# A graph network's three gather passes: block sums by one flat scan over feature-major rows in PSUM instead of chained steps

## Chip, core and metric

The kernel runs on 1 core of one Trainium2 chip. The metric is the device time of one execution in microseconds (us); the program before takes 11177.78 us, the median of 3 runs. Engines: PE is TensorE (matmul), DVE VectorE, ACT ScalarE, POOL GpSimd, SP SyncE.

## The reference

Four residual layers with a layer norm after each, over a graph of 12500 nodes with 64 features and 200000 edges, sorted by their destination `dst`. The last two layers gather rows by `src` and sum them by `dst`, which is what the three passes of this study do:

```
def gcn_conv(x, edge_index, W, b, num_nodes):        # layer 3, twice: passes c1 and c2
    norm = dinv[src] * dinv[dst]
    h = x @ W
    msg = h[src] * norm[:, None]
    out = jax.ops.segment_sum(msg, dst, num_segments=num_nodes)
    return out + b
# layer 4, attention with 4 heads of 16: pass at
attn = a_src_node[src] + a_dst_node[dst] + e_score
attn = jnp.where(attn >= 0, attn, NEG_SLOPE * attn)
attn_max = jnp.zeros((n, H), attn.dtype).at[dst].max(attn)
attn = jnp.exp(attn - attn_max[dst])
attn_sum = jnp.zeros((n, H), attn.dtype).at[dst].add(attn)
attn = attn / (attn_sum[dst] + EPS_SOFTMAX)
msg = h[src] * attn[:, :, None]
out = jnp.zeros((n, H, HD), h.dtype).at[dst].add(msg).reshape(n, OUT_DIM)
```

## The kernel before, in words

The sorted edges are cut into 128 runs, one per partition, of 1568 edges each. A pass goes through its run in NBLK = 98 blocks of J = 16 edges. Since edges of one destination are neighbours, a segment sum is a running sum that a flag resets: `same_dst` holds 1 where an edge has the destination of the edge before it, else 0, and a state is `old * flag + row`. The states of all edges go to DRAM (`states_c`, `states_at`), and after the pass POOL fetches, for each node, the state of its last edge.

The engines of passes c1 and c2 (D = 64 features), and of at (W3 = 68: 4 heads of 16 features and a 17th column, which carries the score and then the exponential; W3S = 72 with the running maximum of each head):

- **POOL** (line 641) issues 16 indirect DMAs a block, each of which gathers one row of the table per partition into `gb[r]`, one of R = 4 buffers. It takes a buffer again when the counter `state` says that the block that was there is summed.
- **DVE**, passes c1 and c2 (`conv`, line 1495): 16 SCALAR_TENSOR_TENSOR a block, each 128x64, each waiting for the one before by the semaphore `chain`; they write `st[h]`, and the last one counts up `state`. DVE itself starts a block when its 16 gathers have landed.
- **DVE**, pass at: L1616 to L1625 copy the maxima out, scale the state carried over and weigh the gathered rows by the exponentials (1024 elements a partition, in place in SBUF). `sums_of` then sums the 16 rows of 68 by a tree of joins (line 1425, 33 short instructions a block), with `run`, products of flags prepared before pass c1 (L1526, L1528). Between its levels stand the steps of the next block's scores (`score_step`, L1582 to L1605), two of which are short scans (L1597, L1601) with the flag rows `msk`.
- **ACT**, pass at: the edges' turned attributes (L689), `msk` (L681) and the exponentials (L701, L703), both in SBUF. In c1 and c2 ACT has nothing to do.
- **SP** (line 507) stores each block's states when `state` allows.

At a pass's end POOL waits for the stores, fixes the rows at the run borders (L599, L603) and fetches the nodes' rows (L610). Before pass at, DVE makes four scans over 1568 elements (L1563).

## Time and profile before

| what | us |
|---|---|
| time, median of 3 runs (lowest, highest) | 11177.78 (11177.54, 11199.18) |
| the profiled execution, span from first to last instruction | 11181.7 |
| busy in that span: POOL / DVE / PE / ACT | 7106.9 / 4736.9 / 1801.6 / 1142.1 |
| pass c1, from 3850 to 6018 | 2168 |
| pass c2, from 6222 to 8390 | 2168 |
| pass at, from 8707 to 10967 | 2260 |

A pass is counted from the start of its first gather to the end of its last. The profile lists no other time of the profiled execution than its span, which lies 3.9 us above the median. The three passes are 6596 us of the 11182; of the rest, about 3850 us are before c1 and are not touched.

### The profile page before, as it was taken

How to read it: one execution, taken by the hardware profiler on the slowest of the kernel's cores; microseconds unless marked ns; L12 is line 12 of the kernel's file. 1: busy time of each engine (PE TensorE's matmuls, PEld its weight loads, DVE VectorE, ACT ScalarE, POOL GpSimd, SP SyncE). 2: the span in 40 equal slices, each digit the busy share in tenths (PEclk: the TensorE clock that was granted, in tenths of full speed). 3: DMA queues.
4: the chain of work that ended last, by engine and by line, in shares of the span. 5: the costliest groups of instructions: out<-in, count | busy, mean ns of one | idle time of the engine just before them, and what ended most of it. 6: DMA issues, size and time to landing. Idle time of an engine off the chain costs nothing.

```text
span 11181.7 us, 57120 instructions
## 1 busy us (share of the span) xinstructions
PE 1801.6 (16%) x9285; PEld 1516.5 (14%) x9285; DVE 4736.9 (42%) x20005; ACT 1142.1 (10%) x2728; POOL 7106.9 (64%) x6884
## 2 busy tenths in 40 slices
PE   8744444444000400000000000000001000000000
PEld 7633333333000300000000000000000000000000
DVE  8855555555797422222221222222224344444446
ACT  0143434343000100000000000000000000000000
POOL 0566666666201377777776677777777776666766
PEclk7755555555555555555555555555555555555555
DMA  5144444444575111111111111111111222222221
GB/s 224 57 129 122 129 124 126 124 127 122 204 273 203 32 50 46 48 46 48 46 48 37 50 46 48 46 48 46 48 46 30 54 53 58 53 58 55 56 55 44
DMA packets 570444, 911.29 MB, mean 81 GB/s; under 512 B 333435, under 2 KB 348228, under 8 KB 544824
## 3 DMA queue, kind: packets, MB, share of 16 engines
q1 hardware_dynamic: 350264, 652.74, 17.3%
q0 software_dynamic: 219904, 255.88, 10.8%
q14 instruction: 226, 1.85, 0.1%
q8 instruction: 50, 0.82, 0.0%
HBM read 494.12 MB, written 414.02 MB: 81 GB/s over the span
## 4 chain that ended last, share of the span: by engine, by line
DVE 34%; issue 28%; another core or an unknown queue 17%; POOL 16%; PE 3%; DMA 1%; ACT 1%; DVEq 0%; SPq 0%; POOLq 0%; ACTq 0%
DVE arena_a L1495 16%; POOL arena_a L641 15%; DVE arena_b L1112 4%; DVE arena_a L1110 3%; DVE arena_b L1125 3%; DVE arena_a L1425 3%; POOL arena_a L610 2%; PE bank L811 2%; DVE arena_b L1056 1%; DVE arena_b L1093 1%; PE bank L916 1%; DVE arena_a L1625 0%; PE bank L890 0%; DMA arena_a<-in_a 0%
## 5 line engine op out<-in xcount | busy, mean ns | idle before, releaser
L641 POOL DMA_INDIRECT arena_a<-table_c,decay x3136 | 3284.6, 1047 | 1257.6 <-issue 1051.2
L1495 DVE SCALAR_TENSOR_TENSOR arena_a<-arena_a,same_dst 128x64 f32<-128x64 f32 x3134 | 891.5, 284 | 3449.5 <-DVE arena_a L1495 2713.2
L591 POOL DMA_INDIRECT by_src<-arena_b,idx_blk x1568 | 1570.8, 1002 | 885.8 <-issue 449.4
L641 POOL DMA_INDIRECT arena_a<-table_at,decay x1568 | 1556.8, 993 | 703.8 <-issue 468.4
L1110 DVE SCALAR_TENSOR_TENSOR arena_a<-arena_a,same_dst 128x64 f32<-128x64 f32 x1567 | 441.9, 282 | 711.1 <-remote 547.7
L864 PE MATMUL bank<-ident,chunk_end 128*64 128x128 f32 (+2 forms) x8 | 2.7, 442 | 4416.0 <-DVEq L973 4416.0
L864 PEld LDWEIGHTS bank<-ident,chunk_end 128*64 128x64 f32 (+2 forms) x8 | 1.4, 240 | 4416.6 <-DVEq L973 4416.6
L1112 DVE SCALAR_TENSOR_TENSOR arena_b<-arena_a,src_f,before 128x128 bf16<-128x128 f32 x1568 | 543.7, 347 | 37.4 <-issue 37.4
L850 PE MATMUL bank<-hrows 98*128 98x128 f32 x1568 | 404.0, 440 | 659.5 <-DVE arena_b L1125 331.9
L850 PE MATMUL bank<-hrows,arena_a 98*128 98x128 f32 x1568 | 403.3, 438 | 658.0 <-DVE arena_b L1125 347.4
L753 ACT ACTIVATE arena_b<-arena_a,decay 128x64 f32<-128x64 f32 x1568 | 394.2, 334 | 972.5 <-remote 610.2
L1215 DVE SCALAR_TENSOR_TENSOR arena_a<-arena_a,mask_blk,hrows 128x96 f32<-128x96 f32 x1567 | 489.5, 312 | 7.4 <-DVE arena_a L1220 4.4
L850 PEld LDWEIGHTS bank<-hrows 98*128 98x128 f32 x1568 | 348.7, 327 | 711.6 <-DVE arena_b L1125 313.8
L850 PEld LDWEIGHTS bank<-hrows,arena_a 98*128 98x128 f32 x1568 | 347.3, 326 | 710.6 <-DVE arena_b L1125 329.6
L1125 DVE SCALAR_TENSOR_TENSOR arena_b<-bank,arena_b 128x128 bf16<-128x128 f32 x1568 | 380.7, 287 | 107.9 <-issue 107.1
L599 POOL DMA_INDIRECT fix_rows<-states_src,fix_from_src x1 | 1.0, 957 | 668.3 <-DMA states_src<-arena_a 668.3
L811 PE MATMUL bank<-arena_b 128*98 128x128 bf16 x3136 | 406.5, 299 | 26.9 <-DVE arena_b L1056 24.9
L943 PE MATMUL bank<-ident,arena_a 128*128 128x128 f32 x196 | 67.4, 447 | 2124.3 <-DMA arena_a<-in_a 1141.4
L1220 DVE SCALAR_TENSOR_TENSOR arena_a<-arena_a,cap_blk,hrows 128x32 f32<-128x32 f32 x1567 | 384.8, 246 | 0.0
L811 PEld LDWEIGHTS bank<-arena_b 128*98 128x98 bf16 x3136 | 365.0, 174 | 68.9 <-DVE arena_b L1056 68.6
L571 POOL DMA_INDIRECT x_at_start<-x,start_i x98 | 143.4, 1464 | 276.3 <-DVEq L973 246.7
L943 PEld LDWEIGHTS bank<-ident,arena_a 128*128 128x128 f32 x196 | 28.7, 205 | 2137.2 <-DMA arena_a<-in_a 1148.7
(279 smaller groups left out, 4845.9 us busy)
## 6 DMA issues: line engine op xcount, KB each, us to landing
arena_a<-ids_rows SPq DMA_DIRECT2D x98, 1024.0 KB
states_src<-arena_a SPq DMA_DIRECT2D x98, 1024.0 KB
states_c<-arena_a SPq DMA_DIRECT2D x196, 512.0 KB
hrows<-by_src SPq DMA_DIRECT2D x98, 776.0 KB, 6.1
states_at<-arena_a SPq DMA_DIRECT2D x98, 576.0 KB
x_at_start<-arena_a SPq DMA_DIRECT2D x7, 7168.0 KB, 49.0
arena_a<-x_at_start SPq DMA_DIRECT2D x98, 512.0 KB
arena_a<-table_c,decay POOLq DMA_INDIRECT x3136
```

The lines of the kernel that those rows point to most:

```text
L591: pool.indirect_dma_start(out=by_src, out_offset=AT(ap=idx_blk[r][:, k:k + 1], axis=0), in_=rows[r][:, k, :], in_offset=None)\
L641: pool.indirect_dma_start(out=gb[r][:, k * w:(k + 1) * w], out_offset=None, in_=table[g], in_offset=AT(ap=src_i[:, n * J + k:n * J + k + 1 ...
L753: ins = act.activation(rows[n % R][:, k, 0:D], xb[n % 2][:, k, :], ACT.Copy, scale=decay[:, t:t + 1])
L811: last = pe.matmul(hist[k % streams], one(oh_hi[h], k), one(oh_lo[h], k), start=False, stop=False)
L850: last = pe.matmul(p_cnt[q][:, k % Q * P:(k % Q + 1) * P], hi_t[h][:, at], snap[h][:, at], start=True, stop=True)
L1110: v.scalar_tensor_tensor(out=xb[h][:, k, :], in0=old, scalar=same_dst[:, t:t + 1], in1=xs[h][:, k, :], op0=ALU.mult, op1=ALU.add).then_inc ...
L1112: rank = v.scalar_tensor_tensor(out=junk[t % 2], in0=ids_in[h][:, k * P:(k + 1) * P], scalar=src_f[:, t:t + 1], in1=before[:, :], op0=ALU. ...
L1125: chosen = v.scalar_tensor_tensor(out=junk[2 + k % Q], in0=p_cnt[q][:, k % Q * P:(k % Q + 1) * P], scalar=1.0, in1=one(oh_lo[h], k), op0=A ...
L1215: xk = c2.done(v.scalar_tensor_tensor(out=new[:, 0:WS], in0=old[:, 0:WS], scalar=mask_blk[:, q, k:k + 1], in1=tb[h][:, k, 0:WS], op0=ALU.m ...
L1220: ins = v.scalar_tensor_tensor(out=new[:, WS:W01], in0=old[:, WS:W01], scalar=cap_blk[:, q, k:k + 1], in1=tb[h][:, k, D:WS], op0=ALU.min, ...
L1425: return v.scalar_tensor_tensor(out=made[:, k, :], in0=old, scalar=scalar, in1=raw[:, k, :] if first else made[:, k, :], op0=ALU.mult, op1 ...
L1495: ins = v.scalar_tensor_tensor(out=st[h][:, k * D:(k + 1) * D], in0=old, scalar=same_dst[:, e:e + 1], in1=gb[r][:, k * D:(k + 1) * D], op0 ...
```

## The change

All three passes sum a block by one TENSOR_TENSOR_SCAN with multiply and add over a flat row. The row is feature-major: for each feature its 17 slots, slot 0 the state carried over, slots 1 to 16 the edges. A mask row of the same form has 0 in slot 0, which starts each feature afresh, and the flags in the others.

- **c1, c2.** ACT (`conv_act`) spreads the flags over the 64 features into `mask{h}` in SBUF (`mask_spread`), turns the gathered rows of the block into `in{h}` in PSUM (`row_turned`), and puts the sums of the block before back edge by edge into `st[h]` (`rows_back`, which counts up `state`). DVE copies the carried state to slot 0 and scans 1088 elements: mask from SBUF, rows from PSUM, sums to SBUF. POOL takes a buffer again on `row_turned`.
- **at.** DVE weighs the rows out of `gb[r]` by exponentials in PSUM (bank 7) into `in0` in PSUM, and scans 1156 elements. ACT writes the exponentials to PSUM, and spreads the mask, whose first 68 elements the two score scans also use, and puts the sums back. POOL takes a buffer again on `weighed`. Score steps 1 and 2 stand before the scan, 3 to 6 behind it.
- `run`, `msk`, `tmp` and `ex` go; two memsets of the masks, 1156 elements each, stand before c1. The PSUM places of the turned attributes and of the scores move to banks 3 to 6.

```diff
                 for n in range(NBLK):
-                    if n >= R:
-                        pool.wait_ge(s("state"), upto(g, "state") + n - R + 1)
+                    if n >= R and g == "at":
+                        pool.wait_ge(s("weighed"), n - R + 1)
+                    elif n >= R:
+                        pool.wait_ge(s("row_turned"), upto(g, "row_turned") + n - R + 1)
...
+        def mask_spread(act, g, n):
+            w = W3 if g == "at" else D
+            if n >= 2:
+                act.wait_ge(s("summed"), upto(g, "summed") + n - 1)
+            act.activation(features(f"mask{n % 2}", w)[:, :, 1:J + 1], bf(same_dst[:, n * J:(n + 1) * J], w), ACT.Copy)\
+               .then_inc(s("mask_spread"), 1)
+        def rows_back(act, g, n):
+            w, row = (W3, W3S) if g == "at" else (D, D)
+            act.wait_ge(s("summed"), upto(g, "summed") + n + 1)
+            if n >= 2:
+                act.wait_ge(s(f"stored{n % 2}"), upto(g, f"stored{n % 2}") + 16 * (n // 2))
+            act.activation(st[n % 2][:, 0:J * row].rearrange("p (j f) -> p j f", f=row)[:, :, 0:w],
+                           features(f"sums{n % 2}", w)[:, :, 1:J + 1].rearrange("p f j -> p j f"), ACT.Copy)\
+               .then_inc(s("state"), 1)
+        def conv_act(act, g):
+            act.wait_ge(s("masks_zeroed"), 1)
+            for n in range(NBLK):
+                r = n % R
+                mask_spread(act, g, n)
+                act.wait_ge(s(f"gathered{r}"), upto(g, f"gathered{r}") + (n // R + 1) * (16 * J))
+                act.activation(features(f"in{n % 2}", D)[:, :, 1:J + 1],
+                               gb[r][:, 0:J * D].rearrange("p (j f) -> p f j", f=D), ACT.Copy)\
+                   .then_inc(s("row_turned"), 1)
+                if n:
+                    rows_back(act, g, n - 1)
+            rows_back(act, g, NBLK - 1)
...
             def conv(g):
-                        ins = v.scalar_tensor_tensor(out=st[h][:, k * D:(k + 1) * D], in0=old,
-                                                     scalar=same_dst[:, e:e + 1],
-                                                     in1=gb[r][:, k * D:(k + 1) * D], op0=ALU.mult, op1=ALU.add)
+                        ins = v.tensor_copy(carried, features(f"sums{1 - h}", D)[:, :, J])
+                    v.tensor_tensor_scan(by_feature[f"sums{h}"][:, flat], by_feature[f"mask{h}"][:, flat],
+                                         by_feature[f"in{h}"][:, flat], 0.0, ALU.mult, ALU.add).then_inc(s("summed"), 1)
...
-                v.tensor_tensor(hview, hview, ex_e.rearrange("p j (c o) -> p j c o", o=1)
+                v.tensor_tensor(weighed(n)[:, :, 0:HD, 1:J + 1].rearrange("p c d j -> p j c d"),
+                                by_head(g3)[:, :, :, 0:HD], ex_e.rearrange("p j (c o) -> p j c o", o=1)
                                 .to_broadcast([P, J, HEADS, HD]), ALU.mult).then_inc(s("weighed"), 1)
...
-                sums_of(n, g3, late["tmp"], s3[:, :, 0:W3], n + 1 if ahead else None)
+                if n >= 2:
+                    v.wait_ge(s("state"), upto("at", "state") + n - 1)
+                v.tensor_tensor_scan(by_feature[f"sums{h}"], by_feature[f"mask{h}"],
+                                     by_feature["in0"][:, 0:W3 * (J + 1)], 0.0, ALU.mult, ALU.add).then_inc(s("summed"), 1)
```

On DVE at the start of pass c1 of the kernel before, `arena_a` holds the gathered rows and the states:

```order
L1477 MEMSET chunk_end 128x128 [waits v_chain]
L1495 SCALAR_TENSOR_TENSOR arena_a<-chunk_end,same_dst,arena_a 128x64 [waits gathered0,v_chain]
L1495 SCALAR_TENSOR_TENSOR arena_a<-arena_a,same_dst 128x64 [waits chain] x15
L1495 SCALAR_TENSOR_TENSOR arena_a<-arena_a,same_dst 128x64 [waits gathered1,state]
L1495 SCALAR_TENSOR_TENSOR arena_a<-arena_a,same_dst 128x64 [waits chain] x15
L1495 SCALAR_TENSOR_TENSOR arena_a<-arena_a,same_dst 128x64 [waits gathered2,state,stored0]
L1495 SCALAR_TENSOR_TENSOR arena_a<-arena_a,same_dst 128x64 [waits chain] x15
```

After the change the same place reads so; what the listing calls SCALAR_TENSOR_TENSOR of 1088 elements is the scan, `banks` is all of PSUM, and the masks lie in `arena_b`:

```order
L1469 MEMSET banks 128x64 [waits v_chain,row_turned]
L1474 SCALAR_TENSOR_TENSOR arena_a<-arena_b,banks 128x1088 [waits mask_spread,row_carried]
L1467 COPY banks<-arena_a 128x64 [waits summed,row_turned]
L1474 SCALAR_TENSOR_TENSOR arena_a<-arena_b,banks 128x1088 [waits mask_spread,row_carried]
L1467 COPY banks<-arena_a 128x64 [waits summed,row_turned,state]
```

A block is 2 instructions on DVE where it was 16.

On DVE in pass at of the kernel before, a piece from the middle of a block (a whole block has 24 such rows, 43 instructions):

```order
L1589 TENSOR_TENSOR arena_a<-arena_a 128x64 [waits gathered0,scores_read]
L1425 SCALAR_TENSOR_TENSOR arena_a<-arena_a,hi_dst 128x68 [waits joined_first]
L1425 SCALAR_TENSOR_TENSOR arena_a<-arena_a,hi_dst 128x68 x3
L1425 SCALAR_TENSOR_TENSOR arena_a<-arena_a,lo_dst 128x68 [waits joined_second]
L1425 SCALAR_TENSOR_TENSOR arena_a<-arena_a,lo_dst 128x68 x3
L1592 SCALAR_TENSOR_TENSOR arena_a<-arena_a 128x16x4 [waits score]
L1425 SCALAR_TENSOR_TENSOR arena_a<-arena_a,lo_dst 128x68 [waits joined_first]
L1425 SCALAR_TENSOR_TENSOR arena_a<-arena_a,lo_dst 128x68 x3
L1597 SCALAR_TENSOR_TENSOR arena_a<-arena_a 128x68 [waits at_mask,score]
L1425 SCALAR_TENSOR_TENSOR arena_a<-arena_a,hi_src 128x68 [waits joined_first,joined_second]
```

After the change a whole block is these 11 instructions; the rows of 1156 (line 1601) and of 68 elements (lines 1564, 1568) are scans:

```order
L1583 COPY arena_a<-arena_a 128x16x4 [waits stored1]
L1590 TENSOR_TENSOR banks<-arena_a,banks 128x68 [waits summed,at_exp]
L1592 TENSOR_TENSOR banks<-arena_a,banks 128x16x4x16
L1549 TENSOR_TENSOR arena_a<-banks,arena_b 128x64 [waits edges_scored]
L1552 COPY arena_a<-arena_a 128x4
L1556 TENSOR_TENSOR arena_a<-arena_a 128x64 [waits gathered0,scores_read]
L1601 SCALAR_TENSOR_TENSOR arena_a<-arena_b,banks 128x1156 [waits state,weighed]
L1559 SCALAR_TENSOR_TENSOR arena_a<-arena_a 128x16x4 [waits score]
L1564 SCALAR_TENSOR_TENSOR arena_a<-arena_b,arena_a 128x68 [waits mask_spread,score]
L1568 SCALAR_TENSOR_TENSOR arena_a<-arena_b,arena_a 128x68 [waits score]
L1572 TENSOR_TENSOR arena_a<-arena_a 128x68 [waits score]
```

The joins are gone, and `state` is waited for by the scan alone.

On ACT in pass c1, where the kernel before has nothing, two blocks now read so (line 704 puts sums back, 695 spreads flags, 715 turns rows):

```order
L704 ACTIVATE arena_a<-arena_a 128x1024 [waits summed]
L695 ACTIVATE arena_b<-same_dst 128x64x16 [waits summed]
L715 ACTIVATE banks<-arena_a 128x64x16 [waits gathered2]
L704 ACTIVATE arena_a<-arena_a 128x1024 [waits summed]
L695 ACTIVATE arena_b<-same_dst 128x64x16 [waits summed]
L715 ACTIVATE banks<-arena_a 128x64x16 [waits gathered3]
```

On ACT in pass at, a block now has these; before, it had L681, L689, L701 and L703, with 64, 256, 68 and 64 elements:

```order
L695 ACTIVATE arena_b<-same_dst 128x68x16 [waits summed]
L728 ACTIVATE arena_a<-banks 128x256 [waits edges_scored,edges_turned]
L738 ACTIVATE banks<-arena_a 128x68 [waits at_args]
L739 ACTIVATE banks<-arena_a 128x4x16
L704 ACTIVATE arena_a<-arena_a 128x16x68 [waits stored0,summed]
```

Three instructions with 1024 elements or more a block come to ACT in c1 and c2, and two in at.

## Rows read from the trace of the kernel before

**Rows 1.** The page: span, and the chain that ended last by engine.
```profile
span 11181.7 us, 57120 instructions
...
DVE 34%; issue 28%; another core or an unknown queue 17%; POOL 16%; PE 3%; DMA 1%; ACT 1%; DVEq 0%; SPq 0%; POOLq 0%; ACTq 0%
```

**Rows 2.** Busy time by stretch: the three gather passes.
```profile
core 0: us, PE busy (x) PEld busy (x) DVE busy (x) ACT busy (x) POOL busy (x), PEclk, DMA share, GB/s
3850.00:6018.00 2168.00, 0.00 (x0) 0.00 (x0) 444.88 (x1561) 0.00 (x0) 1642.07 (x1568) 0.50 0.18 47
...
6222.00:8390.00 2168.00, 0.00 (x0) 0.00 (x0) 440.82 (x1550) 0.00 (x0) 1641.60 (x1568) 0.50 0.18 47
...
8707.00:10967.00 2260.00, 171.01 (x588) 118.97 (x588) 981.24 (x4149) 97.80 (x391) 1556.37 (x1568) 0.50 0.24 57
```

**Rows 3.** Groups by line, POOL's gathers, in 3850:4070, 4092:6018, 8707:10967.
```profile
L641 POOL DMA_INDIRECT arena_a<-table_c,decay x176 | 166.4, 946 | 212.3 <-DMA table_c<-hrows 158.9 <-issue 53.3
...
L641 POOL DMA_INDIRECT arena_a<-table_c,decay x1376 | 1459.5, 1061 | 467.1 <-issue 467.1
...
L641 POOL DMA_INDIRECT arena_a<-table_at,decay x1568 | 1556.8, 993 | 703.8 <-issue 468.4 <-DVE arena_a L1425 160.6 <-remote 74.8
```

**Rows 4.** Groups by line, DVE, 4092:6018.
```profile
L1495 DVE SCALAR_TENSOR_TENSOR arena_a<-arena_a,same_dst 128x64 f32<-128x64 f32 x1376 | 391.2, 284 | 1535.4 <-DVE arena_a L1495 1290.4 <-remote 149.5 <-issue 95.5
```

**Rows 5.** Timeline, early in pass c1.
```profile
3911.54 5.10 DVE L1495 SCALAR_TENSOR_TENSOR arena_a<-arena_a,same_dst 128x64 f32<-128x64 f32 x16 [14.85 <-DMA arena_a<-table_c,decay]
...
3948.99 0.94 POOL L641 DMA_INDIRECT arena_a<-table_c,decay  x1 [0.30 <-issue]
...
3951.56 3.81 DVE L1495 SCALAR_TENSOR_TENSOR arena_a<-arena_a,same_dst 128x64 f32<-128x64 f32 x12 [14.15 <-DMA arena_a<-table_c,decay]
```

**Rows 6.** Timeline, middle of pass c1.
```profile
5018.71 0.28 DVE L1495 SCALAR_TENSOR_TENSOR arena_a<-arena_a,same_dst 128x64 f32<-128x64 f32 x1 [1.13 <-DVE arena_a L1495]
```

**Rows 7.** Timeline, end of pass c1.
```profile
6017.27 1.09 POOL L641 DMA_INDIRECT arena_a<-table_c,decay  x1 [0.30 <-issue]
...
6026.78 0.28 DVE L1495 SCALAR_TENSOR_TENSOR arena_a<-arena_a,same_dst 128x64 f32<-128x64 f32 x1 [1.11 <-DVE arena_a L1495]
...
6042.18 0.28 DVE L1495 SCALAR_TENSOR_TENSOR arena_a<-arena_a,same_dst 128x64 f32<-128x64 f32 x1 [0.41 <-DVE arena_a L1495]
...
6045.88 0.94 POOL L599 DMA_INDIRECT fix_rows<-states_c,fix_from_dst  x1 [27.52 <-DMA states_c<-arena_a]
```

**Rows 8.** Groups by line, DVE, attention pass.
```profile
L1625 DVE TENSOR_TENSOR arena_a<-arena_a 128x1024 f32<-128x1024 f32 x97 | 118.3, 1220 | 0.0
L1597 DVE TENSOR_TENSOR_SCAN arena_a<-arena_a 128x68 f32<-128x68 f32 x97 | 28.5, 294 | 96.5 <-remote 85.0 <-issue 10.9 <-DVE arena_a L1592 0.6
...
L1563 DVE TENSOR_TENSOR_SCAN arena_b<-same_dst,first_adst,arena_b 128x1568 f32<-128x1568 f32 x4 | 13.9, 3486 | 101.3 <-issue 101.2
```

**Rows 9.** Groups by line, ACT, in 2200:3850 and 8707:10967.
```profile
L736 ACT ACTIVATE arena_b<-arena_b,rowno_h 98x2048 bf16<-98x2048 bf16 x25 | 50.5, 2022 | 0.0
...
L689 ACT ACTIVATE arena_a<-bank 128x256 f32<-128x256 f32 x98 | 37.5, 383 | 325.6 <-issue 244.6 <-PE bank L943 81.0
```

**Rows 10.** Timeline: POOL's indirect DMAs beside long DVE instructions.
```profile
8516.61 2.03 DVE L1300 TENSOR_TENSOR x<-x,stat 128x1792 f32<-128x1792 f32 x1
8516.68 2.78 POOL L610 DMA_INDIRECT arena_a<-states_c,end_i_dst  x1 [0.30 <-issue]
...
8520.73 2.02 DVE L1303 TENSOR_REDUCE stat<-arena_b 128x28 f32<-128x1792 f32 x1
8521.82 0.94 POOL L610 DMA_INDIRECT arena_a<-states_c,end_i_dst  x1 [0.30 <-issue]
...
8718.42 3.23 POOL L641 DMA_INDIRECT arena_a<-table_at,decay  x1 [0.31 <-issue]
```

**Rows 11.** Timeline, attention pass, a stall of POOL and what follows.
```profile
8829.67 0.94 POOL L641 DMA_INDIRECT arena_a<-table_at,decay  x1 [12.26 <-DVE arena_a L1425]
...
8830.92 1.41 POOL L641 DMA_INDIRECT arena_a<-table_at,decay  x1 [0.31 <-issue]
```

More of the change, by code:

```diff
@@ L55 @@
     "table_out": 16 * len(PARTS),
-    "onehots": 2 * NB, "onehots_used": 2 * NB, "flag": 1, "flagrow": 1, "chain": (J - 1) * NBLK,
+    "onehots": 2 * NB, "onehots_used": 2 * NB, "flag": 1, "flagrow": 1, "row_turned": NBLK, "row_carried": NBLK, "mask_spread": NBLK, "summed": NBLK,
 }
@@ L59 @@
 ORDER = dict.fromkeys(ADDED, PASSES)
-ORDER.update(dict.fromkeys((*(f"gathered{r}" for r in range(R)), "table", "table_out", "chain"),
-                           CONVS))
+ORDER.update(dict.fromkeys((*(f"gathered{r}" for r in range(R)), "table", "table_out", "row_turned", "row_carried",
+                            "mask_spread", "summed"), CONVS))
 ORDER.update(dict.fromkeys(("onehots", "onehots_used"), ("dst", "src")))
@@ L324, in program @@
         p_small = bank[7]
[L325 to L326 removed]
+        p_turned = [bank[3 + h][:, 0:J * E16] for h in range(2)]
+        p_score = [bank[5 + h][:, 0:J * HEADS] for h in range(2)]
+        p_ex = bank[7][:, 0:HEADS * (J + 1)]
         S = {}
@@ L1476, in conv @@
             def conv(g):
-                link(v.memset(chunk_end[:, :], 0.0))
-                chained = upto(g, "chain")
                 for n in range(NBLK):
-                    h, r = n % 2, n % R
+                    h = n % 2
                     if n >= 2:
-                        v.wait_ge(s(f"stored{h}"), upto(g, f"stored{h}") + 16 * (n // 2))
+                        v.wait_ge(s("state"), upto(g, "state") + n - 1)
+                    v.wait_ge(s("row_turned"), upto(g, "row_turned") + n + 1)
@@ L1503, in conv @@
-                assert chained == upto(g, "chain") + ADDED["chain"]
+                        v.wait_ge(s("summed"), upto(g, "summed") + n)
+                        ins = v.tensor_copy(carried, features(f"sums{1 - h}", D)[:, :, J])
+                    else:
+                        ins = v.memset(carried, 0.0)
+                    ins.then_inc(s("row_carried"), 1)
+                    v.wait_ge(s("row_carried"), upto(g, "row_carried") + n + 1)
+                    v.wait_ge(s("mask_spread"), upto(g, "mask_spread") + n + 1)
@@ L1521, in conv_nodes @@
                 link(v.tensor_tensor(rows3, rows3, per_node(dinv, p, D), ALU.mult))
-            for span, product in run.items():
-                uppers = same_dst[:, :].rearrange("p (m two k) -> p m two k", two=2, k=span)[:, :, 1, :]
-                to = product.rearrange("p n (m k) -> p (n m) k", k=span)
-                link(v.tensor_copy(to, uppers))
-                for k in range(1, span):
-                    link(v.tensor_tensor(to[:, :, k], to[:, :, k], to[:, :, k - 1], ALU.mult))
+            for h in range(2):
+                link(v.memset(by_feature[f"mask{h}"], 0.0))
+            tell("masks_zeroed")
             conv("c1")
@@ L1565, in _ @@
             link(v.memset(late["mx"], 0.0))
-            for h in range(2):
-                link(v.memset(msk[h], 0.0))
             tell("at_begun")
```

128 lines of the change are left out of this document (35 added, 93 removed).

## The prediction

> **What bounds the kernel now.** I read the page's chain first: DVE 34%, issue 28%, an unknown queue 17%, POOL 16% [rows 1]. That is an average over stages, so I cut the time by pass. In c1 and c2 neither engine is busy for the whole 2168 us: DVE 445, POOL 1642, TensorE 0 [rows 2]. The reader is to see that what lies between instructions decides.
>
> POOL: in the first 11 blocks of c1 its 176 gathers took 166.4 us and 53.3 us of idle, "issue": 1.248 us a gather, 19.97 us a block. From 4092 on, 1376 gathers (86 blocks) took 1459.5 + 467.1 = 1926.6 us, 1.400 each, 22.40 a block [rows 3]. DVE in the same stretch: 1376 steps, 391.2 busy + 1535.4 idle = 1926.6, also 1.400 each, 0.28 of work and 1.12 of wait, most of it ended by the step before [rows 4, 6]. The two go in step. Which one leads? Early in c1 DVE ran 16 steps in 5.10 us, then waited 14.85 us for rows, so then POOL led; two blocks later only 12 steps went at that rate [rows 5], and by the middle of the pass all stand 1.40 apart. After the last gather POOL is idle, and DVE still takes 1.40 us for many a step; its last one ends 25 us after that gather starts [rows 7]. So the slow one is DVE: issuing one short instruction and its wait on the chain costs it up to 1.40 us, whatever POOL does, and 16 chained steps make 22.4 us where POOL needs 19.97. POOL is held because `state` frees its buffers. The longer gathers (mean 1.061 for 0.946) I read as an effect of a DVE step that falls into each.
>
> Pass at has 2260 us = 23.06 a block. POOL's gathers are short again (mean 0.993), but it waits 160.6 us for DVE's joins and 74.8 us for a releaser not seen [rows 3]; one such stall is 12.26 us [rows 11]. Here too DVE falls behind by slow issue (981 us busy of 2260 [rows 2]).
>
> **The change, part by part.** *What DVE has left in c1 and c2.* A copy of 64 elements, at most the 0.28 us of a step [rows 4], and a scan. Its price from two scans of this kernel: 1568 elements 3.486 us, 68 elements 0.294 [rows 8]: (3.486 - 0.294)/1500 = 2.13 ns an element, so 1088 elements 2.47 us, 1156 elements 2.61. With a copy, 2.7 us of work; if each of 2 instructions and 3 further waits cost 1.40 us of issue, 7.0 more: under 10 of POOL's 19.97. *What ACT gets.* From 2048 elements at 2.022 us and 256 at 0.383 [rows 9]: 0.91 ns an element, 1024 elements 1.1 us, three of them 3.3. Their views are strided or broadcast, which no row prices; at twice that 6.6 us, plus up to 8 issues of 1.40 = 18 at the worst, still under POOL's block. I cost both at nothing, hidden by the gathers; without that cover one block's chain (turn 1.1, scan 2.5, back 1.1) would show, and it does once, at the end. *Buffers* come free after the turn, two or three us behind the last landing, with three more buffers filling: POOL never waits.
>
> So c1 and c2 go at 1568 x 1.248 = 1957.4 us for 2168: **210.6 us each, 421.2**.
>
> *The tail of c1 and c2.* Now POOL's L599 starts 28.6 us behind the last gather's start (6017.27 to 6045.88), 3.4 us of it the last store (6042.46 to 6045.88) [rows 7]. After: landing 2.6 us from a gather's start (3948.99 to 3951.56 [rows 5]), turn 1.1, scan 2.5, back 1.1, store 3.4, and 1.5 for waits: 12.2. **16.4 each, 32.8**.
>
> *Pass at.* DVE's block: weighing 1.22 [rows 8], scan 2.61, and nine short instructions (maxima, carried state, seven score steps), of which the two score scans, 0.29 each, are the longest kind [rows 8]; I take 0.24 for one, 2.2: 6.0 us in 11 instructions for 43. I count 4 further waits. In a slow stretch, 15 x 0.70 (half of a 1.40 step, which is an instruction with its wait) + 6.0 = 16.5 us, and ACT's two exponentials of 64 to 68 elements, which stand in the chain, at 0.3 each, with three issues of 0.70 2.7 us: 19 us. That is close under POOL's 20; a gain only if it stays so. ACT itself has 2 x 1.1 + 0.4 + 0.6 = 3.2 us. I take it that POOL sets the pace. A block is then 19.97 us at least; at most 20.6, from today's mean: the four long first gathers apart, (1556.8 - 4 x 3.22)/1564 = 0.987, + 0.30, x 16 = 20.6. Part of that comes from the weighing, beside which a gather took 1.41 [rows 11]; both its inputs lie in SBUF now, one will after. I choose 20.15. The first block keeps four gathers of 3.22 us beside the scans of L1563 [rows 8, 10]: 19.97 + 4 x 2.28 = 29.1. Pass: 29.1 + 97 x 20.15 = 1983.7 for 2260: **276.3**. Its tail has a turn less and a rows-back more; I put nothing on it.
>
> *Prepared work.* The flag products and the masks' memsets stand before c1 where DVE waits for the first rows anyway, as it waits 14.85 us for a block early in c1 [rows 5]: nothing.
>
> Sum: 421.2 + 32.8 + 276.3 = 730.3; 11181.7 - 730.3 = 10451.4 for the span; the median lies 3.9 below: **10447.5 us**, ratio 0.935.
>
> **A row and a rule.** Does a scan hold POOL? Beside a TENSOR_TENSOR with both inputs in SBUF POOL's DMA took 2.78 us for 0.94; beside a TENSOR_REDUCE with one input it took 0.94; beside L1563's scans, two inputs in SBUF, 3.23 [rows 10]. The new scans and the weighing have one input in SBUF and one in PSUM, a kind that no long row here shows beside a gather. I take it as the one-input kind, for PSUM is another memory; the other end is priced below as rival B.
> The Trainium skill, page "SBUF — State Buffer", section "Who interferes with whom", says that a DVE instruction with two SBUF inputs contends with a GpSimd instruction that reads SBUF, and one with at most one SBUF input, outside the two-port modes, does not. By that rule the new scans cost POOL nothing, and the sum stands; were a PSUM input no help, it would be 11,000 (rival B at 65%). The rows agree as far as they reach; it also says that descriptor generation needs only the write side, by which L1563 should not have held the gathers, and there the rows (3.23 us) say otherwise.
>
> **Rivals.** *A: pass at stays at DVE's pace.* For it: the 19 us above are near 20, and issue has cost up to 1.40 (15 x 1.40 + 6.0 = 27). Against it: 11 instructions for 43, and today's fast blocks. At 21.5 us a block, + 97 x 1.35 = 131: 10,580; at today's 23.06, + 282: 10,730. *B: the scans hold POOL.* L1563: 2.28 us lost of each 3.49, 65%. In c 0.65 x 2.47 = 1.6 a block, in at 0.65 x (2.61 + 1.22) = 2.5: 196 x 1.6 + 97 x 2.5 = 556 lost: 11,003. If POOL loses their full time, 196 x 2.47 + 97 x 3.83 = 856: 11,303, slower than before. It decides from 730/856 = 85% of the DVE time. For it: the scans of L1563; against: 65% is what they took, and the PSUM input. *C: the 1.40 in c is POOL's own* after some blocks: then c gains nothing, 10447.5 + 421 = 10,869. For it: POOL's longer gathers; against: 1.40 us steps on DVE with POOL idle [rows 7].
>
> **How the numbers follow.** POOL's pace in all passes: 0.69, own range 10,410 to 10,520 (block of at 19.97 to 20.6, + 44; the tails). A 0.17, to 10,730. B at about 65% 0.04, about even 0.02, full 0.05. C 0.03. Range 10,410 to 10,740: the likeliest and A, less what of them falls outside. Faster by over 0.2%, which is what a measurement of this kernel can tell: 0.69 + 0.17 + 0.04 + 0.03 = 0.93; same 0.02; slower 0.05.
>
> **What would show it.** Right: gathers with a median of 0.94 us all through c1 and c2, 1957 us for 1568 of them, POOL's idle time there "issue" alone; scan rows of 2.5 and 2.6 us; 0.94 gathers beside them; POOL's wait before L599 about 11 us for 27.5; no stalls over 1 us in pass at. Wrong: gathers of 2 to 3 us beside scans (B); POOL waiting for `weighed` in at (A), for ACT's turn in c (ACT's copies far above 2 us); gathers still 1.10 us with DVE nearly idle (C).

## The result, and the profile after

The changed kernel took 11106.38 us (median of 4 runs, 11103.41 to 11109.76) against 11185.37 us of the kernel before (median of 4, 11177.54 to 11199.18): ratio 0.9925, 95% interval 0.991 to 0.9939. It is faster, by 79 us or 0.75%, where 730 were forecast (11177.78 to 10447.5 us). The measured time lies 366 us above the upper end of the range (10,410 to 10,740).

The page of the changed kernel, span and chain by engine, in place of [rows 1]:

```profile
span 11101.6 us, 52391 instructions
...
issue 41%; POOL 29%; DVE 19%; another core or an unknown queue 7%; PE 3%; DMA 0%; DVEq 0%; ACT 0%; SPq 0%; POOLq 0%
```

Busy time by stretch, the same columns as [rows 2]:

```profile
3849.00:6018.00 2169.00, 0.00 (x0) 0.00 (x0) 261.06 (x195) 461.49 (x291) 1595.61 (x1568) 0.50 0.19 47
...
6216.00:8385.00 2169.00, 0.00 (x0) 0.00 (x0) 260.98 (x194) 460.37 (x290) 1595.17 (x1568) 0.50 0.19 47
...
8706.00:10888.00 2182.00, 171.33 (x588) 119.24 (x588) 544.19 (x1074) 357.91 (x487) 1607.84 (x1568) 0.50 0.26 59
```

The reader is to see that DVE's work fell (445 to 261 us in c1, 981 to 544 in at), that ACT took 461 us a pass, and that c1 and c2 did not get shorter by it: c1 takes 2168.4 us from the first gather's start to the last one's end, and took 2168.3. Groups by line of POOL's gathers, in the first 11 blocks of c1, in its other blocks, and in pass at, beside [rows 3]:

```profile
L652 POOL DMA_INDIRECT arena_a<-table_c,decay x176 | 166.5, 946 | 212.8 <-DMA table_c<-hrows 159.4 <-issue 53.4
...
L652 POOL DMA_INDIRECT arena_a<-table_c,decay x1376 | 1412.5, 1026 | 514.0 <-issue 514.0
...
L652 POOL DMA_INDIRECT arena_a<-table_at,decay x1568 | 1607.9, 1025 | 573.9 <-issue 573.9
```

Stretch 4092 to 6018: 1412.5 + 514.0 = 1926.5 us for 1376 gathers, 1.400 us each and 22.40 us a block, the very number of before, though DVE had 2 instructions a block in place of 16. Pass at: 2181.8 us for 1568, 22.40 us a block after its first ones, for 23.06. All the idle time is "issue" now.

The timeline of c1, a block among the first eleven and one behind them:

```profile
4052.71 2.42 DVE L1474 TENSOR_TENSOR_SCAN arena_a<-arena_b,banks 128x1088 f32<-128x1088 f32 x1
4052.97 0.94 POOL L652 DMA_INDIRECT arena_a<-table_c,decay  x1 [0.30 <-issue]
...
4206.76 2.42 DVE L1474 TENSOR_TENSOR_SCAN arena_a<-arena_b,banks 128x1088 f32<-128x1088 f32 x1
4206.98 0.95 POOL L652 DMA_INDIRECT arena_a<-table_c,decay  x1 [0.30 <-issue]
...
4208.76 1.94 POOL L652 DMA_INDIRECT arena_a<-table_c,decay  x1 [0.84 <-issue]
4211.56 1.24 POOL L652 DMA_INDIRECT arena_a<-table_c,decay  x1 [0.86 <-issue]
4213.10 0.95 POOL L652 DMA_INDIRECT arena_a<-table_c,decay  x1 [0.31 <-issue]
```

In the early block the gather beside the long scan takes 0.94 us. In the later one, gathers beside the same scan take 0.95 too, and then come one of 1.94 and one of 1.24 us with 0.84 and 0.86 us of idle before them; the next is normal. That is 2.4 us more, once a block, from about the 181st gather of a pass on (181st in c1, 182nd in c2, 183rd in at). Before the change a block had the same 2.4 us more, 0.15 us a gather on average [rows 3], but spread over most of its gathers: two of three took 1.09 us or more in place of 0.94, as the one in [rows 7].

The whole difference of the spans, 80.1 us, falls so (starts of the first gathers and ends of the last ones, before and after): up to c1 0.9 gained; c1 0.1 lost; c1 to c2 204.4 to 198.9 us, 5.5 gained; c2 unchanged; c2 to at 316.6 to 321.8, 5.1 lost; at 2260.3 to 2181.5, 78.8 gained; the end 214.3 to 214.2, 0.1 gained.

### The profile page after: what moved, and what is told of

It is laid out like the page before. It is cut to its first block, busy times and chain, and to the rows that moved or that the text cites. A ratio compares the mean times of both kernels' runs of the same rounds, so it can differ in the third digit from the quotient of the medians.

```text
span 11101.6 us, 52391 instructions
## 1 busy us (share of the span) xinstructions
PE 1806.3 (16%) x9285; PEld 1519.3 (14%) x9285; DVE 3925.1 (35%) x14109; ACT 2341.2 (21%) x3414; POOL 7062.6 (64%) x6884
## 4 chain that ended last, share of the span: by engine, by line
issue 41%; POOL 29%; DVE 19%; another core or an unknown queue 7%; PE 3%; DMA 0%; DVEq 0%; ACT 0%; SPq 0%; POOLq 0%
POOL arena_a L652 27%; DVE arena_b L1152 4%; DVE arena_a L1150 3%; DVE arena_b L1165 3%; DVE arena_a L1260 2%; DVE arena_a L1255 2%; PE banks L851 2%; DVE arena_b L1096 1%; DVE arena_b L1133 1%; POOL arena_a L619 1%; POOL adst_at_start L633 1%; PE banks L956 1%; PE banks L930 0%; POOL by_src L600 0%
## 5 line engine op out<-in xcount | busy, mean ns | idle before, releaser
L652 POOL DMA_INDIRECT arena_a<-table_at,decay x1568 | 1607.9, 1025 | 573.9 <-issue 573.9
L715 ACT ACTIVATE banks<-arena_a 128x1024 f32<-128x1024 f32 x196 | 369.6, 1886 | 3420.3 <-DMA arena_a<-table_c,decay 3420.3
L1150 DVE SCALAR_TENSOR_TENSOR arena_a<-arena_a,same_dst 128x64 f32<-128x64 f32 x1567 | 439.7, 281 | 692.4 <-remote 543.7
L704 ACT ACTIVATE arena_a<-arena_a 128x1024 f32<-128x1024 f32 (+1 forms) x294 | 597.9, 2034 | 3.9 <-DVE arena_a L1601 2.0
L890 PE MATMUL banks<-hrows 98*128 98x128 f32 x1568 | 404.3, 440 | 657.8 <-DVE arena_b L1165 340.8
L890 PE MATMUL banks<-hrows,arena_a 98*128 98x128 f32 x1568 | 402.3, 438 | 658.0 <-DVE arena_b L1165 350.3
L1474 DVE TENSOR_TENSOR_SCAN arena_a<-arena_b,banks 128x1088 f32<-128x1088 f32 x196 | 474.4, 2420 | 6.7
L890 PEld LDWEIGHTS banks<-hrows 98*128 98x128 f32 x1568 | 348.9, 328 | 709.9 <-DVE arena_b L1165 322.8
L890 PEld LDWEIGHTS banks<-hrows,arena_a 98*128 98x128 f32 x1568 | 346.6, 325 | 710.3 <-DVE arena_b L1165 332.5
L608 POOL DMA_INDIRECT fix_rows<-states_src,fix_from_src x1 | 1.0, 957 | 668.6 <-DMA states_src<-arena_a 668.6
L1165 DVE SCALAR_TENSOR_TENSOR arena_b<-banks,arena_b 128x128 bf16<-128x128 f32 x1568 | 381.3, 285 | 118.0 <-issue 117.1
L851 PE MATMUL banks<-arena_b 128*98 128x128 bf16 x3136 | 406.8, 299 | 26.7 <-DVE arena_b L1096 23.1
```

The costliest lines, as they stand in the source:

```text
L652: pool.indirect_dma_start(out=gb[r][:, k * w:(k + 1) * w], out_offset=None, in_=table[g], in_offset=AT(ap=src_i[:, n * J + k:n * J + k + 1 ...
L704: act.activation(st[n % 2][:, 0:J * row].rearrange("p (j f) -> p j f", f=row)[:, :, 0:w], features(f"sums{n % 2}", w)[:, :, 1:J + 1].rearr ...
L715: act.activation(features(f"in{n % 2}", D)[:, :, 1:J + 1], gb[r][:, 0:J * D].rearrange("p (j f) -> p f j", f=D), ACT.Copy)\
L851: last = pe.matmul(hist[k % streams], one(oh_hi[h], k), one(oh_lo[h], k), start=False, stop=False)
L890: last = pe.matmul(p_cnt[q][:, k % Q * P:(k % Q + 1) * P], hi_t[h][:, at], snap[h][:, at], start=True, stop=True)
L1150: v.scalar_tensor_tensor(out=xb[h][:, k, :], in0=old, scalar=same_dst[:, t:t + 1], in1=xs[h][:, k, :], op0=ALU.mult, op1=ALU.add).then_inc ...
```

## Experiments

The experiments ran on six occasions, each with its own runs of the kernel before. These came at two levels, the same program each time: 11,109 to 11,114 us on three occasions, 10,088 to 10,090 on the other three. The first measurement, at 11,185, belongs to the upper ones. All runs of one occasion were at one level. No number below can be read without saying which; I call them the **upper** and the **lower level**. One chip was met at both.

Three words are used from here on. POOL is *held* where its gathers take longer, or start later, than the 0.94 us and 0.30 us between of the first blocks. Its *pace* is the average time from gather to gather that a long pass settles at. The *stock* is what it gains by running faster than that pace at the start of a pass, before it is held.

The first four kernels tested what holds POOL, and fell on the lower level. They start from the changed one unless said:

**e1**: in c1 ACT and DVE handle 1 of 64 features, in c2 SP stores 16 elements a partition and block in place of 1024.
```diff
+WORK = {"c1": 1, "c2": D}      # features turned, scanned, put back
...
-                sp.dma_start(rows_of(states[g], w)[:, bass.ds(blk(i, h) * (J * w), J * w)],
-                             st[h][:, 0:J * w]).then_inc(s(f"stored{h}"), 16)
+                kept = 16 if g == "c2" else J * w
+                sp.dma_start(rows_of(states[g], w)[:, bass.ds(blk(i, h) * (J * w), kept)],
+                             st[h][:, 0:kept]).then_inc(s(f"stored{h}"), 16)
```


> From the changed kernel. In pass c1 ACT and DVE turn, scan and put back 1 of the 64 features (stores whole); in pass c2 they do all 64, but SP stores 16 elements a partition for a block in place of 1024 (the nodes' rows are then fetched from the states of c1). After the change both passes show 11 blocks of 20.0 us and 87 of 22.40, with one place a block where gathers take 1.94 and 1.24 us. Theory POOL (its indirect DMAs have a lasting pace of 1.40 us each, whatever the other engines do): both passes unchanged, about 2166 us each. Theory burst (ACT's and DVE's long instructions hold POOL once a block): c1 at 98 x 20.0 = 1960 us, c2 unchanged. Theory store (SP's store holds it): c2 at 1960, c1 unchanged.

**e2**: 64 rows a gather in c1, 8 gathers a block in c2.
```diff
+GATHERS = {"c1": J, "c2": J // 2, "at": J}
...
+                    given = P // 2 if g == "c1" else P
+                    for k in range(GATHERS[g]):
+                        pool.indirect_dma_start(out=gb[r][0:given, k * w:(k + 1) * w], out_offset=None, in_=table[g],
+                                                in_offset=AT(ap=src_i[0:given, n * J + k:n * J + k + 1], axis=0))
```


> From the changed kernel. In pass c1 each gather fetches 64 rows (partitions 0 to 63) in place of 128; in pass c2 a block issues 8 gathers in place of 16. Theory POOL with a pace per instruction: c1 unchanged at 2166 us, c2 at 98 x 8 x 1.40 = 1098 us less the stock at the start of some 27 us, so 1071 to 1098. Theory POOL with a pace per row (descriptor): c1 far shorter, at 1.25 us a gather or less (1960 us or less). Theory of something that comes once a block: c2 at 98 x (8 x 1.25 + 2.4) = 1215 us.

**e3**: POOL pauses before every fourth block in c1, before every block in c2, until ACT has turned the rows of the block before.
```diff
+                    elif n and (g == "c2" or n % 4 == 0):
+                        pool.wait_ge(s("row_turned"), upto(g, "row_turned") + n)
```


> From the changed kernel. In pass c1 POOL waits, before every fourth block, for the turned rows of the block just before, in c2 before every block; each such wait idles it some 4.4 us (2.45 us to land, 1.9 to turn). Theory of a lasting pace with a stock (idle time fills it again): in c1 the pauses cost nothing beyond the 22.40 us a block (4 x 20.0 + 4.4 = 84.4 is under 4 x 22.4 = 89.6), so about 2166 us, or down to 2066 if idle time counts for more than itself; in c2 blocks of 20.0 + 4.4 = 24.4 us with gathers of 0.95 throughout, 2391 us. Theory of a hold that comes with each block from the twelfth on: c1 at 2166 + 24 x 4.4 = 2272, c2 at 2166 + 97 x 4.4 = 2593.

**e4**: the kernel before with 8 of 16 chained steps, the other rows left out (and e1's small stores in c2).
```diff
-                    for k in range(J):
+                    for k in range(STEPS):      # STEPS = 8
```


> From the kernel before. DVE does 8 of the 16 chained steps of a block in c1 and c2 (the other rows are left out); in c2 SP also stores 16 elements a partition for a block (nodes' rows are fetched from the states of c1). The prediction's theory (DVE's 16 steps of 1.40 us hold POOL through the counter that frees buffers): 8 steps need 11 us at most, so both passes fall to 98 x 19.97 = 1957 us. Theory POOL (1.40 us a gather is its own lasting pace): both passes stay at about 2166 us, 22.40 a block after some 11 blocks.

Measured, kernel before 10089.79: e1 10000.51, e2 8966.44, e3 10415.54, e4 10076.15 us. c1 and c2 took 1957 us in e1 and 1958 in e4; e2's gathers of 64 rows went at 1.205 us each; e3's pauses cost some 3.4 us each (c1 2038, c2 2282), not the 4.4 expected. Nothing is held on this level, so nothing was told apart. That the kernel before took 1,088 us less than at first was the surprise. Next, both kernels unedited:

> The kernel before, unedited, for its trace. In the four runs behind this call's predecessor it took 10089.79 us, 1088 less than the 11177.78 of the first measurement, and POOL's gathers there had a median of 0.944 us throughout. Theory of a chip or a condition of it: passes c1 and c2 at 98 x 19.97 = 1957 us where the total is near 10,090, and at 2166 where it is near 11,180; the lasting pace of 1.40 us a gather is then not in the program.

> The changed kernel, unedited, against the kernel before. Theory of a chip or a condition of it: where the kernel before takes some 10,090 us, c1 and c2 are at POOL's 19.97 us a block in both kernels, and the change gains only its tails (16 us a pass) and what pass at loses to DVE, together 0 to 100 us, ratio 0.99 to 1.0. Where the kernel before takes 11,180, as first measured: ratio 0.9925.

Upper level: before 11109.01, change 11041.57, ratio 0.9935 (0.9918 to 0.9951). The kernels of e1 to e4 were then run again:

> The kernel of e1 once more (c1: 1 of 64 features turned, scanned and put back; c2: stores of 16 elements a partition), wanted on a chip where the kernel before takes about 11,100 us, for on the first chip it ran at 19.97 us a block everywhere and told nothing apart. If the kernel before takes 11,100 here: theory POOL (1.40 us a gather is the pace of its indirect DMAs on that chip) both passes 2166 us; theory burst c1 1960; theory store c2 1960. If it takes 10,090: both 1957 again.

> The kernel of e2 once more (c1: gathers of 64 rows; c2: 8 gathers a block). If the kernel before takes 11,100 us here: theory of a pace per instruction c1 2166, c2 1071 to 1098; per row c1 at 1.205 us a gather, 1889 us, as on the first chip; theory of a hold once a block c2 1215. If it takes 10,090: 1889 and 979 again.

> The kernel of e3 once more (a pause of some 4.4 us before every fourth block in c1, every block in c2). If the kernel before takes 11,100 us here: theory of a lasting pace with a stock that idle time fills: c1 about 2066 to 2166, c2 near the 2282 of the first chip; theory of a hold with each block: c1 2272, c2 2500 or more. If it takes 10,090: 2038 and 2282 again.

> The kernel of e4 once more (the kernel before with 8 of 16 chained steps; small stores in c2). If the kernel before takes 11,100 us here: the prediction's theory (DVE's steps hold POOL) 1957 us a pass; theory POOL 2166 a pass. If it takes 10,090: 1958 again.

Upper level (kernel before 11108.87): e1 11041.55, e2 9949.59, e3 11136.35, e4 11101.71 us. e4, groups by line of POOL and DVE in c1 from 4092 on:

```profile
L646 POOL DMA_INDIRECT arena_a<-table_c,decay x1332 | 1372.1, 1030 | 492.2 <-issue 492.2
...
L1500 DVE SCALAR_TENSOR_TENSOR arena_a<-arena_a,same_dst 128x64 f32<-128x64 f32 x664 | 189.3, 285 | 1669.7 <-DMA arena_a<-table_c,decay 1648.8
```

This is the answer to the prediction's question of who leads. DVE does its 8 steps back to back in 2.53 us and waits for rows for 1649 of 1864 us; POOL's gathers still stand at (1372.1 + 492.2)/1332 = 1.400 us, and c1 and c2 take 2167.6 and 2167.2 us. The theory that DVE's steps hold POOL has fallen. e1's pass c1, POOL and what ACT does for rows (0.2 us where the changed kernel has 1.9):

```profile
L659 POOL DMA_INDIRECT arena_a<-table_c,decay x1568 | 1631.7, 1041 | 695.6 <-issue 535.7 <-DMA table_c<-hrows 159.8
...
L723 ACT ACTIVATE banks<-arena_a 128x16 f32<-128x16 f32 x97 | 19.4, 200 | 2104.0 <-DMA arena_a<-table_c,decay 2104.0
```

c1 2167.4 us, c2 with small stores 2167.4: neither the work of ACT and DVE nor the store. e2, c1 and c2:

```profile
L658 POOL DMA_INDIRECT arena_a<-table_c,decay x1568 | 1596.0, 1018 | 730.0 <-issue 571.2 <-DMA table_c<-hrows 158.8
...
L658 POOL DMA_INDIRECT arena_a<-table_c,decay x784 | 811.3, 1035 | 316.1 <-issue 259.9 <-DMA table_c<-hrows 56.2
```

Gathers of 64 rows: 2167.2 us, as with 128, although each takes 0.90 us at its shortest: the pace does not go by rows or bytes. 784 gathers: 1071.2 us, inside the 1071 to 1098 of the expectation, and not the 1215 of a hold once a block. So the pace is one of gathers: 1.40 us each, after a stock worth some 27 us (1568 x 1.400 - 2168). e3 (c1):

```profile
L654 POOL DMA_INDIRECT arena_a<-table_c,decay x1568 | 1562.7, 997 | 764.1 <-issue 517.4 <-DMA table_c<-hrows 158.9 <-ACT banks L717 87.9
```

24 pauses, 88 us waited for ACT, and the pass takes 2168.0 us as without them: time that POOL spends idle builds up the stock again. Pauses in every block (c2) gave 2285.1 us, 3 more than on the lower level: a pass whose blocks take over 22.40 us anyway hardly meets the hold. (Blocks of 24.4 us were expected; with pauses of 3.4 they took 23.3.)

Does every instruction count against the pace, or every one that counts up a semaphore? **e5** puts memsets on POOL:
```diff
+                        if g in ("c1", "c2") and k % 2:
+                            col = ((g == "c2") * NBLK * J + n * J + k) // 2
+                            ins = pool.memset(extra[:, col:col + 1], 0)
+                            if g == "c2":
+                                ins.then_inc(s("extra"), 1)
```


> From the changed kernel. POOL sets one byte a partition to zero behind every second gather: 8 memsets a block more, in c1 without a semaphore, in c2 each counting up a semaphore of its own (some 0.1 us of work each). Runs so far: on three chips with the kernel before at about 11,100 us POOL's gathers have a lasting pace of 1.40 us each, alike for 64 and 128 rows, and 784 of them took 1071 us; on one chip with 10,090 us there is none (1.25). If this chip is of the first kind: pace per indirect DMA, c1 and c2 at 2166 to 2170; pace per instruction that counts up a semaphore, c1 2166, c2 98 x 24 x 1.40 less 27 = 3270 us; pace per instruction of any kind, both 3270. If of the second kind: 1957 + 784 x 0.1 = 2035 in both or a little more.

Lower level: 10019.59, c1 and c2 1957 us; the memsets cost nothing, where 2035 was expected. Again as e5b, with **e8**, which puts 16 memsets behind DVE's scan:

> The kernel of e5 once more (8 memsets a block more on POOL, in c1 without a semaphore, in c2 counting one up); the last call's runs were all in the fast condition (kernel before at 10,090 us), where they cost nothing. If the kernel before takes 11,100 here: pace per indirect DMA, c1 and c2 2166 to 2170 us; pace per instruction that counts up a semaphore, c1 2166, c2 3270; pace per instruction of any kind, both 3270.

```diff
+                    for k in range(EXTRA):      # 16
+                        ins = v.memset(extra[:, n * EXTRA + k:n * EXTRA + k + 1], 0)
+                        if g == "c1":
+                            ins.then_inc(s("extra"), 1)
```


> From the changed kernel. DVE sets 16 bytes a partition a block to zero behind its scan, 16 memsets; in c1 each counts up a semaphore of its own, in c2 none does. DVE has then 18 instructions a block that count up in c1, and 2 in c2. If the kernel before takes 11,100 us here: theory of a lasting pace of 1.40 us for each instruction that counts up (on DVE as on POOL), c1 at 98 x 25.2 less some 27 = 2440 us with DVE late, c2 at 2166; theory of a pace per instruction of any kind, both 2440; theory of a pace of POOL's DMAs alone, with DVE's slow steps a matter of the chained waits of the kernel before, both 2166. If it takes 10,090: both 1957, the memsets cost under 3 us of DVE's time a block.

> The changed kernel, unedited, against the kernel before. With the kernel before at 11,100 us: ratio 0.993 as twice before. At 10,090: c1 and c2 at 1957 us in both kernels, pass at 2040 before and 1967 after (as in e7), tails worth 5 to 15 us more: 70 to 85 us under it, ratio 0.992.

Upper level (before 11114.17): e5b 11056.26, e8 11082.2, the change 11038.96 (ratio 0.9931, 0.9914 to 0.9948). e5b, POOL in c1 and in c2:

```profile
L653 POOL DMA_INDIRECT arena_a<-table_c,decay x1568 | 1479.0, 943 | 740.1 <-issue 579.5 <-DMA table_c<-hrows 159.6
L658 POOL MEMSET extra<- 128x1 uint8 x784 | 92.1, 117 | 42.8 <-issue 42.4
...
L653 POOL DMA_INDIRECT arena_a<-table_c,decay x1568 | 1479.1, 943 | 632.7 <-issue 586.0 <-DMA table_c<-hrows 45.8
L658 POOL MEMSET extra<- 128x1 uint8 x784 | 92.2, 118 | 34.5 <-issue 33.8
```

c1 2191.9, c2 2190.0 us: some 24 us more than without memsets, above the 2166 to 2170 of the first form and far from the 3270 of the others, with a semaphore or without. The pace goes neither by POOL's instructions nor by those that count up: it is 2191.9/1568 = 1.398 us a gather. What the memsets took is the stock: POOL's idle times grow from the 57th gather of c1 and the 64th of c2, not from the 181st. No gather of c1 and c2 took over 0.961 us here; the hold lies in the idle time alone. e8 (timeline, places in c1 and one in c2):

```profile
5001.65 0.94 POOL L654 DMA_INDIRECT arena_a<-table_c,decay  x1 [0.30 <-issue]
5001.66 0.06 DVE L1481 MEMSET extra<- 128x1 uint8 x1 [1.34 <-issue]
5002.90 0.95 POOL L654 DMA_INDIRECT arena_a<-table_c,decay  x1 [0.30 <-issue]
5003.06 0.06 DVE L1481 MEMSET extra<- 128x1 uint8 x1 [1.34 <-issue]
...
5023.11 0.94 POOL L654 DMA_INDIRECT arena_a<-table_c,decay  x1 [5.53 <-issue]
...
7184.03 0.94 POOL L654 DMA_INDIRECT arena_a<-table_c,decay  x1 [0.30 <-issue]
7184.04 0.06 DVE L1481 MEMSET extra<- 128x1 uint8 x1 [1.34 <-issue]
7185.27 0.94 POOL L654 DMA_INDIRECT arena_a<-table_c,decay  x1 [0.30 <-issue]
7185.44 0.06 DVE L1481 MEMSET extra<- 128x1 uint8 x1 [1.34 <-issue]
```

c1 2190.2, c2 2187.5 us. At these places memsets of 0.06 us stand 1.40 us apart on DVE, in c1, where each counts up, and in c2, where none does; the blocks at both take 25.20 us, which is DVE's 18 instructions at 1.40, and the gathers beside take 0.94 us with 0.30 between, but for one pause of 5.5 us a block. In c1 DVE is held from its fourth block on; from 4097 to 4702 POOL is held as well, at 22.4 us a block on average, while DVE falls behind it; from 4727 on POOL has no free buffer left, pauses, and its gathers are short again. So the hold falls on DVE's issue as well as on POOL's, with a semaphore or without. A lasting pace of DVE it is not: 98 blocks of 18 instructions in 2190 us are 1.24 us each, and in some stretches its blocks take 17.5 us. The gathers again come to the pace that POOL has everywhere on this level, 2190.2/1568 = 1.397 us, with the stock all but gone. None of the three forms that I had put down forecast 2190 in both passes (2440 in c1 alone, 2440 in both, 2166 in both). The cause of the hold stays open.

**e7** takes the change apart: c1 and c2 as before (`conv` with its 16 steps, POOL waiting for `state`, ACT idle), pass at changed.
```diff
-                if p == len(PARTS) - 1 and g in ("c1", "c2"):
-                    conv_act(act, g)
...
-                        pool.wait_ge(s("row_turned"), upto(g, "row_turned") + n - R + 1)
+                        pool.wait_ge(s("state"), upto(g, "state") + n - R + 1)
```


> From the changed kernel, with c1 and c2 put back to the kernel before (DVE's 16 chained steps a block, POOL waiting for the summed block); the attention pass stays changed. The first two traces differ by 78.8 us in pass at, and by 1 us or less in c1 and c2; a tail saves 16 us behind each, of which 5 reached the next pass in one case and none in the other. So, on a chip with the kernel before at 11,100: 60 to 80 us under it, ratio 0.993 to 0.9945, nearly all of the change's gain. If the gain were from c1 and c2: 0 to 20 us. On a chip with 10,090: pass at 2038 before, 1967 after, so 70 us under it as well, ratio 0.993.

> The kernel of e7 once more (c1 and c2 as before the change, the attention pass changed). With the kernel before at 11,100 us: pass at 2176 for 2238 us, c1 and c2 unchanged, 55 to 70 us under the kernel before, ratio 0.994 to 0.995. At 10,090: 70 us again.

> The changed kernel, unedited, in the same session as e7b. With the kernel before at 11,100: 70 us under it, within 15 us of e7b. At 10,090: 75 to 100 us under it, so 5 to 30 more than e7b, the tails of c1 and c2 (some 12 us each, the first half used up by what follows).

Both times it was the lower level. First: e7 10019.72 against 10089.96, ratio 0.9929 (0.9912 to 0.9946). Then: e7b 10017.22, the whole change 10012.16, before 10088.26; ratios 0.9928 (0.9912 to 0.9945) and 0.9924 (0.9908 to 0.9941). So 71 us come from pass at and 5 us from c1 and c2 together; the intervals of the two overlap, so that the 5 stand on the medians alone. No run has this kernel on the upper level. Pass c1 of e7b from 3466 on, POOL and the 16 steps of before:

```profile
L652 POOL DMA_INDIRECT arena_a<-table_c,decay x1562 | 1477.4, 946 | 475.9 <-issue 475.9
...
L1475 DVE SCALAR_TENSOR_TENSOR arena_a<-arena_a,same_dst 128x64 f32<-128x64 f32 x1567 | 446.7, 285 | 1499.0 <-DMA arena_a<-table_c,decay 1446.2
```

DVE's steps wait for rows, 0.28 us each and 0.03 apart: the old chain was never late here (the pass takes 1960 us), and the new pass is 1957. Pass at of the change on this level:

```profile
L652 POOL DMA_INDIRECT arena_a<-table_at,decay x1568 | 1489.6, 950 | 477.8 <-issue 477.8
```

1967.1 us; e4, which has the pass of before, took 2038. On the upper level the unedited kernels took 2176 and 2238 when run again, 62 us apart, for the 78.8 of the first pair (its kernel before took 76 us more in all, 57 of them ahead of c1 and 22 in pass at).

## Why the prediction was wrong

**The step that failed** is "Which one leads? ... the slow one is DVE". From it came 421 of the 730 us. On the upper level POOL has a lasting pace of 1.40 us a gather of its own (e4b: half the steps, same 22.40; e2b: half the gathers, half the time). DVE's 16 steps stood 1.40 us apart too, as e8's memsets do in stretches; that the same hold made both is likely, not shown. Both gave 22.4 us a block: I took an equality of two engines for a chain between them. Two rows that I had spoke against it. A wait for a freed buffer comes once a block, before its first gather; but of the 2.4 us that a block had over 19.97, 16 x (1061 - 946) ns = 1.8 us lay in the gathers' own durations, and the idle time was all "issue" [rows 3]. (The trace has the rest, 0.86 us of idle for 0.30, before the fifth gather of every block, not the first.) I called that an effect. And DVE's slow steps with POOL idle [rows 7] said that DVE was slow, not that POOL would be fast.

**c1 and c2**: forecast 210.6 each, measured none (0.05 lost, 0.04 gained). Where the pace is absent, POOL does go at 19.97 us a block as forecast, but it does so before the change too, since DVE's steps then take 5 us a block.

**Tails**: right in size, small in worth. Forecast 12.2 us from the last gather to L608, in the order below; the timeline of the changed kernel gives 12.6 (6016.53 to 6029.16), for 28.6 before [rows 7]:

```profile
6016.53 0.94 POOL L652 DMA_INDIRECT arena_a<-table_c,decay  x1 [0.30 <-issue]
6019.01 1.89 ACT L715 ACTIVATE banks<-arena_a 128x1024 f32<-128x1024 f32 x1 [17.67 <-DMA arena_a<-table_c,decay]
...
6021.29 2.42 DVE L1474 TENSOR_TENSOR_SCAN arena_a<-arena_b,banks 128x1088 f32<-128x1088 f32 x1
...
6023.74 2.02 ACT L704 ACTIVATE arena_a<-arena_a 128x1024 f32<-128x1024 f32 x1 [0.92 <-DVE arena_a L1474]
...
6029.16 0.94 POOL L608 DMA_INDIRECT fix_rows<-states_c,fix_from_dst  x1 [11.69 <-DMA states_c<-arena_a]
```

But the 28.6 was the hold on DVE's last steps: on the lower level the 16 steps of e7b give 11.1 us, less than the 12.6 of the change, so that there is no such gain there. Of the 16.0 us, 5.5 reached c2 and none reached at, where POOL then waited 25.58 us at line 633 for work of the other engines that it had not waited for before. The term left out what stands behind it. The trace shows what made that work late (PE, changed kernel):

```profile
8477.17 0.69 PE L930 MATMUL banks<-ident,x 128*128 128x128 f32 x2 [13.78 <-ACT arena_b L675]
...
8493.97 0.69 PE L930 MATMUL banks<-ident,x 128*128 128x128 f32 x2 [15.26 <-issue]
...
8510.77 0.69 PE L930 MATMUL banks<-ident,x 128*128 128x128 f32 x2 [15.26 <-issue]
...
8527.57 1.22 PE L956 MATMUL banks<-wnode,arena_b 128*128 128x128 f32 x4 [15.26 <-ACT arena_b L675]
```

TensorE's groups of 6 matmuls and 6 weight loads stand 16.80 us apart, 12 x 1.40: the hold falls on TensorE too. It does so between c1 and c2 in both kernels, but between c2 and at only in the changed one. e3b, where POOL had paused in every block of c2, and the lower level show no such gaps there, and c2 to at takes 300.5 and 299.5 us for 321.8.

**Pass at**: forecast 276.3, measured 78.8 (62 when run again, 71 on the lower level). The mechanism was right: POOL's waits for DVE, 160.6 + 74.8 us [rows 3], are gone, and its idle is all "issue". But the gathers then reached the lasting pace: mean 1025 for 993 ns (51 us more), issue 573.9 for 468.4 us (105.5 more); 235.4 - 156.6 = 78.8. The stalls of before had built up the stock, which the fast blocks between them used. The mis-sized term is the block behind the first one: 20.15 forecast, (2181.5 - 29.2)/97 = 22.19 measured. On the lower level it was (1967.1 - 29.0)/97 = 19.98, so that the term was good for a POOL that nothing holds; but there the pass of before took 2038 us, not 2260.

**Prices**: the scans, whole changed kernel:

```profile
L1474 DVE TENSOR_TENSOR_SCAN arena_a<-arena_b,banks 128x1088 f32<-128x1088 f32 x196 | 474.4, 2420 | 6.7
L1601 DVE TENSOR_TENSOR_SCAN arena_a<-arena_b,banks 128x1156 f32<-128x1156 f32 x98 | 250.2, 2553 | 0.4 <-issue 0.4
L1592 DVE TENSOR_TENSOR banks<-arena_a,banks 128x1024 f32<-128x1024 f32 x98 | 119.6, 1221 | 0.0
```

2.42, 2.55 and 1.22 us for 2.47, 2.61 and 1.22. ACT, pass c1:

```profile
L704 ACT ACTIVATE arena_a<-arena_a 128x1024 f32<-128x1024 f32 x96 | 191.7, 1997 | 0.0
L715 ACT ACTIVATE banks<-arena_a 128x1024 f32<-128x1024 f32 x97 | 182.9, 1886 | 1690.7 <-DMA arena_a<-table_c,decay 1690.7
L695 ACT ACTIVATE arena_b<-same_dst 128x1024 f32<-128x1024 f32 x98 | 102.0, 1041 | 3.7 <-DVEq L1013 3.7
```

Turning and putting back take 1.89 and 2.00 us where 1.1 was taken and twice that bounded; the spread of the flags 1.04. Hidden, as said, but for the tail.

**Rivals**: B did not happen, though one row looks like it: the gather of 1.94 us at 4208.76 begins under a scan, and on the upper level this is so in nearly every block of c1 and c2. Yet the first eleven blocks have the same scans and no long gather, e1b with scans of 17 elements is as slow, and on the lower level the changed kernel's gathers in c1 and c2 (min, median, max) never pass 0.961 us beside the full scans:

```profile
L652 POOL DMA_INDIRECT arena_a<-table_c,decay x3136: 938/944/961, 3463.4 to 7533.2; - x196
```

The Trainium skill's rule ("SBUF — State Buffer", "Who interferes with whom"), that a DVE instruction with at most one SBUF input does not contend with GpSimd outside the two-port modes, agrees with that row. C ("the 1.40 in c is POOL's own") is what happened, at 0.03 chance, and I had set its price, 10,869, with pass at unheld. With the pace in pass at too, 29.1 + 97 x 22.40 less the stock of 27 = 2,175 for 1,984 us, it would have come to 11,060, near the 11,106. Its chance was set low by the row on which the failed step rested. No rival had the program itself at two levels; the forecast speaks of the upper one, on which its rows were taken.

## What to carry to other kernels

Before an engine's work is cut, ask what ended the waits of the engine that it is said to hold: a wait that the suspect causes stands where the program waits for it (here once a block), and not in the length of most instructions. Two engines with the same period are no proof that one leads; halve the work of one and look at the other. A stall before a paced engine is not all gain when removed: here a third of it was (79 of 235 us).
